# A router stage in one pass, a third PSUM bank for turned heads, and token lists shared between two engines

## The chip, the cores and the metric

One core of a Trainium2 chip runs the whole program. The metric is the time of one execution on the device, in microseconds (us), as the median of the runs shown; less is better. The core's engines run side by side and meet at semaphores: TensorE (PE, matmuls; PEld is its weight load), VectorE (DVE), ScalarE (ACT), GpSimd (POOL), and SyncE (SP), which here only issues transfers. TensorE's clock has two levels, 2.4 GHz (granted clock 1.0) and 1.2 GHz (0.5).

## What is computed

The reference takes x and a context of 8 batches x 256 tokens x 512 features through four stages. The change touches the first two:

```python
x = x + xattn(layernorm(x), ctx)            # 16 heads of 32; RMS norms on q and k; text part is empty
x = x + moe(layernorm(x))                   # 64 experts, the 8 best of each token
x = x + memory_attention(layernorm(x), ctx, mask)
x = x + ternary_ffn(layernorm(x))           # 512 -> 1408 -> 512

def moe(x):                                 # x: 2048 tokens x 512
    scores = softmax(x @ gate_weight.T)     # 64 scores a token
    topk_w, topk_idx = top_k(scores, 8)
    topk_w = topk_w / sum(topk_w)
    # each token goes to its 8 experts (512 -> 192 -> 512, silu), sorted by expert,
    # and the 8 results come back weighted
```

At the end of the attention the heads' outputs are multiplied by a 512x512 matrix and its bias `o_b` is added. The choice of experts depends on small differences of scores, so matmuls here are in float32, or in several passes of `fp32r` with each operand split into a high and a low part.

## The kernel before

The 2048 tokens are 16 tiles of 128 (`NT` = 16, P = 128), and 512 features are `DC` = 4 chunks of 128. Each stage is a block with one instruction stream for each engine; a barrier stands between blocks. Engines meet through `Steps`: a counter on which `done(instruction, name)` counts up and `wait(engine, unit, name)` waits for a named step of a unit. Each engine runs its own stream strictly in the order in which it is written.

- **project** (lines 89 to 243) makes qT, kT and V for 16 tiles. POOL normalises the tile's rows (L167 to L172) and otherwise waits for PE.
- **attend** (L246) has 32 units (8 batches x 4 groups of 4 heads), each in 2 slots of 2 heads. In slot s PE makes the scores `pS` (L312), in odd slots then the products `pO` of the unit two before (L333), and last it turns the heads of slot s-2 into `pT` (L323, on the page with `ident` as operand). DVE takes the smallest score of a row, `low` (L354), the reciprocals `inv` (L359) and copies three of four turned heads from PSUM (L368). ACT copies the fourth (L381), takes the exponentials `prob` (L388), and in even slots copies `pO` back into qT (L394, called "O"). POOL multiplies the probabilities by `inv` (L405). PSUM: two buffers pS of two banks each, two banks pT (head 0 and 1 of a slot), two banks pO, used by odd and even units. SP writes zeroes to unused rows and makes copies of the last stage's weights in DRAM.
- **route** (L419) has two passes. Pass one: POOL copies a tile of qT (L461), PE multiplies by `Wo` in float32 (L475), DVE adds the bias and then the sum to X and takes its statistics (L528 to L533). After all 16 tiles come the scales of the layernorm (16 aggregates, a root on ACT). Pass two, again over 16 tiles: ACT normalises (L510) into one of two buffers h, which is also stored to DRAM, PE turns h (L484), DVE copies it from PSUM (L546), PE makes 64 logits (L496), and DVE copies them, finds the 8 largest and marks them (L554 to L569). `Wo` and the bias are loaded when the block begins.
- **place** (L573) gives each pair of token and expert a slot in blocks of 128 rows, and makes for each block the list of its tokens: for each tile 8 one-hot matrices `hotr` (row, DVE, L741) and 8 step matrices `hotb` (block, ACT, L671), two buffers each, and 8 matmuls (L653) that wait for both. ACT also makes the high parts of the first three experts' weights (`wgu_high` L800, `wd_high` L805), two before its first step matrix and one after the ninth tile.
- **experts** and **finish** follow. In experts POOL names the first rows and gathers them (L925, L932); both stages are bound to what place and attend leave in memory.

## Time and profile before

| | us |
|---|---|
| median of 3 runs | 1686.16 |
| lowest and highest | 1680.62 and 1689.4 |
| the profiled execution, its own time | 1689.1 |
| its span (first to last instruction) | 1687.3 |

So 1.8 us of the profiled time lie outside its span, and the profiled execution is 2.9 us above the median. A row of a timeline gives start, duration, engine, source line, operation, what is written and read, a count of merged instructions, and in brackets the idle time before it and what ended that. A row of windows gives the stretch, its length, for each engine the busy time (and its instructions), then TensorE's granted clock, the share of time in which the DMA engines were busy, and GB/s. Start-to-start distances count, since the durations of successive instructions overlap by their pipelines.

### The profile page before, as it was taken

To read this page: it belongs to the slowest core of one execution; us is meant where nothing else is said; L and a number is where in the kernel's file an instruction comes from. 1 tells how busy PE (TensorE), PEld (TensorE's weight loads), DVE (VectorE), ACT (ScalarE), POOL (GpSimd) and SP (SyncE) were. 2 spreads that over 40 slices of the span, in tenths; PEclk is the share of its full clock that TensorE was granted. 3 is DMA by queue.
4 is the path that set the end of the run, shared out by engine and by line. 5 is a ranking of instruction groups with operands and counts; after the bars stand their busy time and mean duration, and the time that the engine had idled before them with its cause. 6 is when DMAs were issued, how large, how long until landed. Compare 5 with 4: busy or idle time off the path is not lost. (4 is left out here: it accounts for less than half of the span.)

```text
span 1687.3 us, 38047 instructions
## 1 busy us (share of the span) xinstructions
PE 1486.4 (88%) x8473; PEld 1166.0 (69%) x8474; DVE 1036.2 (61%) x2058; ACT 855.6 (51%) x1955; POOL 596.7 (35%) x680
## 2 busy tenths in 40 slices
PE   2999989998985479999999999999990679999999
PEld 1554556665453368888898899888980468888888
DVE  3343447776468847677767666666654556677632
ACT  0222257887025836576766666666650324444442
POOL 1111036776103132223223222322225476666322
PEclk9999969999986579999999999999995789999999
DMA  5000079000016148787878787777736554444200
GB/s 218 25 19 25 19 278 328 2 1 12 23 64 267 63 128 278 261 272 267 281 261 283 245 277 258 251 260 256 253 124 197 177 157 137 132 135 132 86 13 26
DMA packets 90388, 273.79 MB, mean 162 GB/s; under 512 B 12437, under 2 KB 12566, under 8 KB 89110
## 3 DMA queue, kind: packets, MB, share of 16 engines
q1 hardware_dynamic: 66214, 192.06, 31.9%
q0 software_dynamic: 23680, 77.61, 15.4%
q10 hardware_dynamic: 432, 3.41, 0.5%
q8 instruction: 24, 0.39, 0.1%
q14 instruction: 38, 0.31, 0.1%
HBM read 204.88 MB, written 76.81 MB: 167 GB/s over the span
## 5 line engine op out<-in xcount | busy, mean ns | idle before, releaser
L932 POOL DMA_INDIRECT xg<-h_rows,idx x168 | 184.4, 1098 | 466.2 <-PE m_x L960 457.1
L975 PE MATMUL m_g<-wgu_high,bxTh 128*128 x660 | 236.4, 358 | 4.2 <-DVE bxTl L1048 4.2
L975 PE MATMUL m_g<-wgu_low,bxTh 128*128 x660 | 223.9, 339 | 0.0
L975 PE MATMUL m_g<-wgu_high,bxTl 128*128 x660 | 223.7, 339 | 0.0
L1378 PE MATMUL f_g<-x4T_high,ffn_gu 128*128 128x256 f32 x704 | 176.9, 293 | 13.8 <-issue 12.1
L1378 PE MATMUL f_g<-x4T_low,ffn_gu 128*128 128x256 f32 x704 | 169.8, 282 | 0.0
L1048 DVE TENSOR_TENSOR bxTl<-m_x,bxTh 128x512 fp32r<-128x512 f32 x166 | 114.7, 691 | 84.8 <-ACT bxTh L1117 66.3
L810 DVE TENSOR_TENSOR wgu_low<-raw_gu,wgu_high x61 | 107.3, 1759 | 80.8 <-ACT wgu_high L800 64.5
L1135 ACT ACTIVATE y<-m_y 128x512 f32<-128x512 f32 x164 | 98.3, 599 | 110.7 <-PE m_y L995 89.1
L405 POOL TENSOR_TENSOR prob<-prob,inv 128x512 f32<-128x512 f32 x128 | 130.5, 1041 | 64.0 <-DVE inv L359 63.9
L1269 POOL DMA_INDIRECT G<-y_rows,slot x128 | 133.2, 1040 | 55.4 <-issue 49.4
L995 PE MATMUL m_y<-wd_high,hidTm 128*128 x328 | 144.7, 441 | 7.8 <-issue 6.1
L1378 PEld LDWEIGHTS f_g<-x4T_high,ffn_gu 128*128 128x128 f32 x704 | 135.1, 192 | 19.2 <-issue 16.5
L388 ACT ACTIVATE prob<-pS,low 128x256 f32<-128x256 f32 x256 | 118.0, 473 | 43.2 <-DVE low L354 43.2
L1378 PEld LDWEIGHTS f_g<-x4T_low,ffn_gu 128*128 128x128 f32 x704 | 135.0, 192 | 2.1 <-issue 1.7
L995 PE MATMUL m_y<-wd_low,hidTm 128*128 x328 | 130.1, 397 | 0.0
L975 PEld LDWEIGHTS m_g<-wgu_high,bxTh 128*128 128x128 f32 x660 | 124.5, 189 | 5.4 <-issue 4.6
L975 PEld LDWEIGHTS m_g<-wgu_low,bxTh 128*128 128x128 f32 x660 | 125.1, 189 | 0.0
L975 PEld LDWEIGHTS m_g<-wgu_high,bxTl 128*128 128x128 f32 x660 | 124.8, 189 | 0.0
L1117 ACT ACTIVATE bxTh<-m_x 128x512 fp32r<-128x512 f32 x166 | 99.0, 597 | 43.8 <-issue 42.3
L1432 DVE SCALAR_TENSOR_TENSOR X<-G,w,X 128x512 f32 (+1 forms) x128 | 106.1, 868 | 15.3 <-DMA G<-y_rows,slot 14.7
L1275 POOL TENSOR_TENSOR hT_low<-f_hid,hT_high 128x256 fp32r<-128x256 f32 x88 | 65.9, 750 | 119.5 <-ACT hT_high L1616 118.2
(235 smaller groups left out, 3155.9 us busy)
## 6 DMA issues: line engine op xcount, KB each, us to landing
raw_gu<-in_exp_gu SPq DMA_DIRECT2D x64, 768.0 KB, 6.8
y_rows<-y SPq DMA_DIRECT2D x164, 256.0 KB
raw_d<-in_exp_d SPq DMA_DIRECT2D x64, 512.0 KB, 7.6
y_rows<-zero SPq DMA_DIRECT2D x64, 256.0 KB, 3.4
ffn_gu<-ffn_gu_words SPq DMA_DIRECT2D x1, 5632.0 KB
X<-in_x SPq DMA_DIRECT2D x4, 1024.0 KB, 18.0
ctxT<-in_ctxT SPq DMA_DIRECT2D x16, 256.0 KB, 2.6
h_rows<-h SPq DMA_DIRECT2D x16, 256.0 KB, 2.0
```

Of the source, the lines that this page charges most:

```text
L388: e = eng.activation(prob[:, s % BUFS, i, h, :], pS[s % 2][:, i, h, :], ACT.Exp, bias=low[:, s % BUFS, i, h:h + 1], scale=-1.0, accum_out= ...
L405: poolN.done(eng.tensor_tensor(w, w, inv[:, s % BUFS, i, :].unsqueeze(2).to_broadcast([P, TPB, S]), ALU.mult), f"N{i}")
L810: eng.tensor_tensor(self.gu[1][:, at, :], self.raw_gu[:, at, :], self.gu[0][:, at, :].bitcast(F32), ALU.subtract).then_inc(self.s_low_gu, 1)
L932: eng.indirect_dma_start(xg[:, u, :].bitcast(F32), None, h_dram, bass.IndirectOffsetOnAxis(ap=idx[half][:, u:u + 1], axis=0)).then_inc(s_g ...
L975: m = eng.matmul(pg[u % 2][:, 0:2 * I], xT[l][:, u % 2, c, :], W.gu[r][:, buf * DC + c, :], start=c == 0 and n == 0, stop=c == DC - 1 and ...
L995: m = eng.matmul(py[par][:, :], left, right, start=n == 0, stop=n == 4)
L1048: dveX.done(eng.tensor_tensor(xT[1][:, u % 2, :, :], px[u % 2][:, :].rearrange("p (c n) -> p c n", c=DC), xT[0][:, u % 2, :, :].bitcast(F3 ...
L1117: actX.done(eng.activation(xT[0][:, u % 2, :, :], px[u % 2][:, :].rearrange("p (c n) -> p c n", c=DC), ACT.Copy), "xTh")
L1135: actY.done(eng.activation(y[:, u % 2, :], py[u % 2][:, :], ACT.Copy), "y")
L1269: eng.indirect_dma_start(G[:, i, k, :], None, y_dram, bass.IndirectOffsetOnAxis(ap=slot8[:, t, k:k + 1], axis=0)).then_inc(s_g[i][k], 16)
L1378: m = eng.matmul(pgu[f % 2][:, bass.ts(n, S)], Wgu[:, n, c, bass.ts(f, P)].bitcast(way), x[:, c, :].bitcast(way), start=c == 0 and part == ...
L1432: dveA.done(eng.scalar_tensor_tensor(X[:, t, :], G[:, i, k, :], w8[:, t, k:k + 1], X[:, t, :], ALU.mult, ALU.add), f"k{k}_{i}")
```

## The change

**project**: POOL adds `o_b` to each tile of X (a further `tensor_tensor` of 128x512), and waits for `rows`, now six rows, before it begins.

**attend**: `pT` has three banks, taken in turn by all heads, and `pO` has one bank in place of two. SP first loads the raw output weights; ACT makes their high parts in slots 8 to 11, POOL the low parts in slots 12 to 15.

**route**: one pass of 16 tiles. The product with the output weights is 12 `fp32r` matmuls of 512 columns a tile (high x high, high x low, low x high, for 4 chunks) in place of 4 in float32. ACT makes the high part of a tile of qT, DVE the low part. DVE adds the product to X in one operation, takes the statistics and one aggregate; POOL adds the epsilon and raises to -1/2; DVE makes the shift; ACT normalises (four buffers h) and also takes over the copy of the turned tile. The five operations on the logits stay on DVE.

**place**: `hotr` reads its row of numbers from SBUF in float16, in place of PSUM in float32. Of 8 step matrices DVE makes two for the first 12 tiles and one for the last 4, ACT the others. ACT makes one expert's high parts ahead of the step matrices, the others after tiles 1 and 3.

**experts**: POOL issues its first gathers ahead of the load of the number of used groups.

```diff
@@ project @@
+            eng.wait_ge(s_rows, 16)
...
+                    pool.done(eng.tensor_tensor(X[:, t, :], xc[:, :], rows[:, 5, :], ALU.add), "xb")
@@ attend @@
-        pT = [ps(f"pT{j}", [P, TPB, S]) for j in range(PAIR)]
-        pO = [ps(f"pO{j}", [P, S]) for j in range(2)]
+        pT, pO = [ps(f"pT{n}", [P, TPB, S]) for n in range(TBUFS)], ps("pO", [P, S])
...
+            eng.dma_start(Wraw[:, :, :], a["attn_wT"][3]).then_inc(s_wo, 16)
...
-                    turned(eng, (s - 1) // PAIRS, (s - 1) % PAIRS * PAIR + i)
+                    turned(eng, n - TBUFS)
...
-                actO.wait(eng, u - 2, "O")
+                actO.wait(eng, u - 1, "O")
...
+                if s in HIGHS:
+                    eng.wait_ge(s_wo, 16)
+                    eng.activation(Wo[0][:, s - HIGHS[0], :], Wraw[:, s - HIGHS[0], :], ACT.Copy).then_inc(s_high, 1)
                 if s % PAIRS == 0 and 0 <= s // PAIRS - 3 < UNITS:
                     u = s // PAIRS - 3
                     peO.wait(eng, u, "O")
-                    actO.done(eng.activation(qT[:, u % DC, bass.ts(u // DC, S)], pO[u % 2][:, :], ACT.Copy), "O")
+                    actO.done(eng.activation(qT[:, u % DC, bass.ts(u // DC, S)], pO[:, :], ACT.Copy), "O")
@@ route, TensorE and GpSimd @@
+                for c in range(DC):
+                    for n, (l, r) in enumerate(THREE):
+                        m = eng.matmul(po[t % 2][:, :], oT[l][:, t % 2, c, :], Wo[r][:, c, :],
+                                       start=c == 0 and n == 0, stop=c == DC - 1 and n == 2)
...
+            for s in range(NT + 2):
+                if s == 2:
+                    eng.wait_ge(s_r, 16)
+                if s >= 2:
+                    turn(s - 2)
+                if s < NT:
+                    project_out(s)
+                if s >= 2:
+                    choose(s - 2)
...
+                dveX.wait(eng, t, "mv")
+                actH.wait(eng, t - 2, "h")
+                pool.done(eng.tensor_scalar_add(lnp[:, t % 2, 0:1], mv[:, t % 2, 1:2], LN_EPS), "var")
+                pool.wait(eng, t, "var")
+                pool.done(eng.tensor_tensor(lnp[:, t % 2, 0:1], lnp[:, t % 2, 0:1], minus_half[:, :], ALU.pow), "rstd")
@@ place @@
+        on_vector = lambda t, k: k == K - 1 or (k == K - 2 and t < 3 * NT // 4)
...
-            for n in range(NWB - 1):
-                W.high_gu(eng, n, n)
-                W.high_d(eng, n, n)
+            W.high_gu(eng, 0, 0)
+            W.high_d(eng, 0, 0)
...
-                if t == NT // 2:
-                    W.high_gu(eng, NWB - 1, NWB - 1)
-                    W.high_d(eng, NWB - 1, NWB - 1)
+                if t in (1, 3):
+                    W.high_gu(eng, (t + 1) // 2, (t + 1) // 2)
+                    W.high_d(eng, (t + 1) // 2, (t + 1) // 2)
...
-                    m = eng.tensor_scalar(hotr[:, t % 2, k, :], prow[:, :], row_f[:, t, k:k + 1], tok_half[:, t:t + 1], ALU.is_equal, ALU.mult)
+                    m = eng.tensor_scalar(hotr[:, t % 2, k, :], it_row[:, :], row_f[:, t, k:k + 1], tok_half[:, t:t + 1], ALU.is_equal, ALU.mult)
+                    if on_vector(t, k):
+                        m = eng.tensor_scalar(hotb[:, t % 2, k, :], it_blk[:, :], blk_f[:, t, k:k + 1], 2.0, ALU.is_gt, ALU.mult)
@@ experts, GpSimd @@
-            groups = used_groups(eng, endb)
             name(0, 0)
             name(1, 1)
             for u in range(GB):
                 gather(0, u, 0)
+            groups = used_groups(eng, endb)
```

TensorE's stream in attend, from an odd slot's scores to the next even slot's, before. `a_dveT` and `a_actT` are the copies of turned heads, `a_poolN` the scaled probabilities, `a_actO` the copy of a product:

```order
L312 MATMUL pS1<-kT,qT 128x256 x3
L333 MATMUL pO1<-probT,V 32x256 [waits a_dveT,a_actT,a_actO]
L333 MATMUL pO1<-probT,V 32x256 x7
L323 MATMUL pT0<-ident,prob 128x128 [waits a_dveT,a_poolN]
L323 MATMUL pT1<-ident,prob 128x128 [waits a_dveT,a_poolN]
L312 MATMUL pS0<-kT,qT 128x256 [waits a_actE]
```

The same place in the changed kernel:

```order
L319 MATMUL pS1<-kT,qT 128x256 x3
L341 MATMUL pO<-probT,V 32x256 [waits a_dveT,a_actT,a_actO]
L341 MATMUL pO<-probT,V 32x256 x7
L331 MATMUL pT1<-ident,prob 128x128 [waits a_actT,a_poolN]
L331 MATMUL pT2<-ident,prob 128x128 [waits a_dveT,a_poolN]
L319 MATMUL pS0<-kT,qT 128x256 [waits a_actE]
```

The order is the same; the products go into the one bank `pO` every time, so their wait on `a_actO` is for the copy of the unit just before.

ACT's stream at the same place in the changed kernel (that of before differs only in the numbers of pO and pT):

```order
L396 ACTIVATE prob,tot<-pS0,low 128x256 [waits a_dveR,a_peT,a_dveM]
L396 ACTIVATE prob,tot<-pS0,low 128x256 x3
L405 ACTIVATE qT<-pO 128x256 [waits a_peO]
L396 ACTIVATE prob,tot<-pS1,low 128x256 [waits a_dveR,a_peT,a_dveM]
L396 ACTIVATE prob,tot<-pS1,low 128x256 x3
L389 ACTIVATE probT<-pT0 128x512 [waits a_peO,a_peT]
```

The copy that frees `pO` stands behind the four exponentials of the even slot.

DVE's stream in route, one tile of the second pass, before (`spares` and `low_bits` hold logits, masks and the best eight):

```order
L546 COPY hT<-ph0 128x512 [waits r_peL,r_peH]
L554 COPY spares<-pl1 128x64 [waits r_peL]
L557 MAX low_bits<-spares 128x8 [waits r_dveB]
L561 MATCH_REPLACE rest<-low_bits,spares 128x64 [waits r_dveB]
L563 TENSOR_TENSOR spares<-spares,rest 128x64 [waits r_dveB]
L569 TENSOR_TENSOR spares<-spares 128x64 [waits r_dveB]
```

One tile in the changed kernel:

```order
L572 SCALAR_TENSOR_TENSOR ln2_scale_shift<-ln2_mv,ln2_scale_shift 128x1 [waits r_pool]
L576 COPY spares<-pl1 128x64 [waits r_peL]
L557 TENSOR_TENSOR oT_low<-qT,oT_high 128x512 [waits r_peO,r_actO]
L581 MAX low_bits<-spares 128x8 [waits r_dveB]
L586 MATCH_REPLACE rest<-low_bits,spares 128x64 [waits r_dveB]
L590 TENSOR_TENSOR spares<-spares,rest 128x64 [waits r_dveB]
L598 TENSOR_TENSOR spares<-spares 128x64 [waits r_dveB]
L561 TENSOR_TENSOR X<-po0,X 128x512 [waits r_peO]
L564 BN_STATS ln2_stats<-X 128x6 [waits r_dveX]
L568 BN_AGGR ln2_mv<-ln2_stats 128x2 [waits r_dveS,r_pool,r_dveX]
```

The shift of a tile, which waits for POOL, is the first operation behind that tile's aggregate.

## Rows read from the trace of the kernel before

**Rows 1.** Windows: attend at half and at full clock, route, place.

```profile
219.50:261.70 42.20, 37.54 (x192) 24.28 (x192) 20.36 (x31) 23.39 (x88) 18.63 (x19) 0.56 0.95 356
261.70:418.80 157.10, 149.22 (x1345) 96.52 (x1344) 123.30 (x194) 127.26 (x492) 112.44 (x111) 1.00 0.20 68
418.80:524.60 105.80, 87.99 (x320) 52.82 (x320) 62.39 (x179) 14.30 (x18) 9.81 (x16) 0.88 0.14 54
524.60:594.60 70.00, 27.00 (x135) 17.28 (x135) 62.31 (x215) 54.98 (x138) 23.04 (x21) 0.50 0.44 177
```

**Rows 2.** Timeline of attend at the full clock, one unit of two slots.

```profile
300.57 1.13 PE L312 MATMUL pS<-kT,qT 32*128 32x256 f32 x8
301.75 1.23 DVE L354 TENSOR_REDUCE low<-pS 128x4 f32<-128x1024 f32 x1 [0.82 <-PE pS L312]
302.49 0.63 PE L323 MATMUL pT<-ident,prob 128*128 128x128 f32 x4 [0.21 <-ACT probT L381]
...
304.12 1.07 PE L333 MATMUL pO<-probT,V 128*32 128x256 f32 x16
304.82 0.40 ACT L394 ACTIVATE qT<-pO 128x256 f32<-128x256 f32 x1
305.12 1.09 PE L323 MATMUL pT<-ident,prob 128*128 128x128 f32 x8
306.14 1.13 PE L312 MATMUL pS<-kT,qT 32*128 32x256 f32 x8
```

**Rows 3.** Timeline of attend at the half clock, an odd slot.

```profile
256.40 2.08 PE L312 MATMUL pS<-kT,qT 32*128 32x256 f32 x8
...
258.40 1.94 PE L333 MATMUL pO<-probT,V 128*32 128x256 f32 x16
...
260.27 1.50 PE L323 MATMUL pT<-ident,prob 128*128 128x128 f32 x8
```

**Rows 4.** Timeline of route: pass one's start and one tile, then pass two.

```profile
424.33 25.88 PE L475 MATMUL po<-wo,oT 128*128 128x512 f32 x55 [6.01 <-DMA wo<-in_attn_wT]
...
451.51 0.69 DVE L530 TENSOR_TENSOR X<-X,add 128x512 f32 x1
...
452.44 0.69 DVE L533 BATCH_NORM_STATS2 ln_stats<-X  x1 [0.24 <-DVE X L530]
...
498.51 0.23 DVE L557 MAX8 low_bits<-spares 128x8 f32<-128x64 f32 x1
...
499.57 0.68 DVE L546 COPY hT<-ph 128x512 f32<-128x512 f32 x1
...
500.40 1.10 PE L496 MATMUL pl<-router_w,hT 128*128 128x64 f32 x8 [0.48 <-DVE spares L554]
```

**Rows 5.** Timeline of experts: `fp32r` matmuls of 512 columns.

```profile
702.70 0.39 PE L995 MATMUL m_y<-wd_high,hidTm 128*128 x1
702.93 0.39 PE L995 MATMUL m_y<-wd_low,hidTm 128*128 x1
```

**Rows 6.** Timeline of finish: the same two GpSimd operations on two columns.

```profile
1304.78 0.23 POOL L1281 TENSOR_SCALAR n_lnp<-n_mv 128x2 f32<-128x2 f32 x1
1305.09 0.73 POOL L1283 TENSOR_TENSOR n_lnp<-n_lnp,minus_half 128x2 f32<-128x2 f32 x1
```

**Rows 7.** Timeline of place.

```profile
532.95 0.23 DVE L722 TENSOR_SCALAR step<-blk_f 128x128 f32<-128x128 f32 x1
...
536.12 25.50 ACT L671 ACTIVATE hotb<-it_blk,step 128x201 f16<-128x201 f16 x72
...
549.20 2.64 DVE L741 TENSOR_SCALAR hotr<-prow,row_f,tok_half 128x128 f16<-128x128 f32 x8 [0.18 <-PE plist L653]
...
561.54 1.47 ACT L800 ACTIVATE wgu_high<-raw_gu 128x1536 fp32r<-128x1536 f32 x1
...
563.86 19.84 ACT L671 ACTIVATE hotb<-it_blk,step 128x201 f16<-128x201 f16 x56
```

**Rows 8.** Timeline of experts' start: the first gather.

```profile
596.27 1.23 POOL L932 DMA_INDIRECT xg<-h_rows,idx  x1 [0.89 <-POOL idx L925]
```

More of the change, by code:

```diff
@@ L416, in by_unit, with route @@
         one(t, t % unroll, lambda k, t=t: t + k < n)
-def route(nc, a, h_dram, X, qT, L, mask16, cum16, m8, ident):
+def route(nc, a, h_dram, X, qT, Wo, L, mask16, cum16, m8, ident):
+    tiles, HBUF = range(NT), 4
+    THREE = ((0, 0), (0, 1), (1, 0))
     with ExitStack() as ctx:
@@ L506, in _ @@
-            eng.wait_ge(s_ln, 1)
-            def norm(t, u):
-                peH.wait(eng, t - 2, "hT")
-                act.done(eng.activation(h[:, u, :], X[:, t, :], ACT.Identity, bias=lnp[:, t, 1:2], scale=lnp[:, t, 0:1]), "h")
-            for u in range(2):
-                norm(u, u)
-            with eng.Fori(1, NT // 2) as i:
-                for u in range(2):
-                    eng.wait_ge(s_h[u], i * 16)
-                    norm(i * 2 + u, u)
+            for x in (actO, actH, actT):
+                x.start(eng)
@@ L519, in _, with turned @@
+            def turned(t):
+                peH.wait(eng, t, "hT")
+                peL.wait(eng, t - 2, "l")
+                actT.done(eng.activation(hT[:, t % 2, :, :], ph[t % 2][:, :].rearrange("p (c n) -> p c n", c=DC), ACT.Copy), "hT")
+            high(0)
+            for s in range(NT + 2):
+                if s + 1 < NT:
+                    high(s + 1)
+                if 1 <= s <= NT:
+                    norm(s - 1)
+                if s >= 2:
+                    turned(s - 2)
         @block.vector
@@ L569, in one @@
                     dveB.done(eng.tensor_tensor(cum16[:, t, :], cum16[:, t - 1, :], mask16[:, t, :], ALU.add), "cum")
-            for t in range(NT):
-                one(t, t % 2, lambda k, t=t: t + k < NT)
+            low(0)
+            for s in range(NT + 3):
+                if 1 <= s <= NT:
+                    shift(s - 1)
+                b = s - 3
+                if b >= 0:
+                    logits(b)
+                if s + 1 < NT:
+                    low(s + 1)
+                if b >= 0:
+                    best(b)
+                    others(b)
+                    chosen(b)
+                    counted(b)
+                if s < NT:
+                    residual(s)
 def place(nc, a, W, Wgu, ffn_gu, s_ffn, L, mask16, cum16, m8, slot8, w8, blk_tok, endb, blk_tab, tab_dram):
```

175 lines of the change are left out of this document (87 added, 88 removed).

## The prediction

> **What bounds the kernel now.** I read the windows by stage first: the change touches attend, route and place, and what they take is 42.2 + 157.1, 105.8 and 70.0 us [rows 1]. Then I read the timeline of each, to see which wait ends last there.
>
> In attend at the full clock TensorE is busy in 149 of 157 us [rows 1]. One unit runs from one even slot's scores to the next, 300.57 to 306.14: 5.57 us [rows 2], and the slots from 261.7 on repeat it 26 times up to the last even slot. The only stall the rows show is one of 0.21 us at the second turned head, which waits for ACT's copy out of its bank. The products begin at 304.12, and ACT copies the products of the unit before at 304.82, after it: with two banks nobody minds [rows 2]. In the first 42 us the clock is at its half level (0.56 on average) [rows 1]; there scores take 2.00, products 1.87 (start to start, 256.40, 258.40, 260.27) [rows 3].
>
> In route TensorE bounds pass one and the clock is mostly up (0.88) [rows 1]; the block begins at 418.8 and its first matmul only at 424.33, after 6.01 us of waiting for the weights [rows 4]. In place TensorE is busy in 27 of 70 us at 0.50 [rows 1], and ACT's step matrices come without a gap: 72 in 25.50 us and 56 in 19.84, 0.354 each; DVE takes 2.64 for a tile's eight row matrices against ACT's 2.83 [rows 7].
>
> **attend: one bank for the products.** This is the edit that I take to decide. With one bank, the products of a unit wait for the copy of the unit before, and ACT does that copy behind the four exponentials of the even slot, which wait for `low`, which waits for that slot's scores. And the next even slot's scores stand behind the products on TensorE. That closes a loop, whose length is, from [rows 2]: scores to start of `low` 1.18 (300.57 to 301.75), start of `low` to the copy 3.07 (to 304.82, through the exponentials, without a gap), the copy 0.40, hand-over 0.12, products to turning 1.00 (304.12 to 305.12), turning to the next scores 1.02 (to 306.14). Sum 6.79, against 5.57 now: 1.22 more a unit, 26 times: **+31.7**. It does not depend on how early the heads are turned: nothing in the loop waits for `pT`. What is queued behind the waiting product is everything TensorE does next, the turning of the odd slot and the next scores, and behind those DVE and ACT.
>
> The third bank takes the 0.21 stall away, 26 x 0.21 = 5.5 at best. In the new loop it is worth nothing: there TensorE already has 1.2 us to spare in a unit.
>
> At the half clock the same loop costs 1.18 + 0.95 (scores 2.08 in place of 1.13) + 3.07 + 0.40 + 0.12 + 1.87 and about 1.9 for the turning [rows 2, 3] = 9.5, against 2 x 2.0 + 1.87 + 2 x 1.9 = 9.7 of TensorE's own work in a unit. So the first 42 us stay as they are.
>
> ACT's four high parts: those in slots 9 and 11 are beside the loop, those in 8 and 10 stand in it, ahead of the copy. 512 columns cost 0.5 to 0.6 by the 1536 columns in 1.47 [rows 7]: **+1.0** together. POOL's four low parts fit into its share (112 of 157 us busy [rows 1]), and the load is issued first on SP: 0; without that cover, 1 us each.
>
> **project.** POOL's extra addition lies beside TensorE and is needed only by route: 0. Only the first tile's could delay a matmul, by under 1 us.
>
> **route.** In the new pass a tile costs TensorE 12 x 0.233 = 2.8 [rows 5] for the product, about 0.5 for the turning (eight in 1.02 [rows 2]) and 1.1 for the logits [rows 4]: 4.4. DVE's stream costs more. From its rows [rows 4]: X to statistics 0.93, statistics 0.69, then a wait like the 0.24 there and the aggregate, 1.1 together; the low part 0.7 (the shape of L530); four operations on the logits 1.06 (498.51 to 499.57); the shift and the copy of the logits 0.2 each: 4.2. Then the loop passes POOL: epsilon 0.31 start to start and the power 0.73 [rows 6] and two hand-overs, 1.2, in which DVE stands, since the shift is next in its stream: 5.4 a tile. The power there has two columns, here one; a small POOL operation is 0.23 [rows 6], so the price is between 0.23 and 0.73, I take the row of the same operation, 0.73; the lower end would give 4.9 a tile, 7 us less in all. What is late, then, is DVE's loop, not TensorE.
>
> Sum: to the first aggregate 7.5 (ACT and DVE split the first tile, 1.5; 12 matmuls, 2.8 or 5.1 with the clock down; DVE 2), two tiles without logits at 4.1, 13 at 5.4, and 6.4 from the last aggregate (POOL 1.2, shift, normalising, turning, copy and logits 3.4, the last operations 1.8): 7.5 + 8.2 + 70.2 + 6.4 = 92.3 against 105.8: **-13.5**. The removed weight load (6.01 us [rows 4]) is in it.
>
> **place.** `step` is there at 533.18 [rows 7], and one expert's high parts end about 533.9. ACT then has 12 x 6 + 4 x 7 = 100 step matrices at 0.354 = 35.4 and two more experts at 2.32 (561.54 to 563.86) = 4.6: it ends at 573.9. Now it ends at 563.86 + 19.84 = 583.7: **-9.8**, if DVE keeps up. DVE begins at 536 as now. A row matrix costs 0.33 now, from PSUM; a float32 operation of 128 columns from SBUF takes 0.23 [rows 7]. At 0.23 for the row and 0.27 for the step matrix (201 columns) DVE needs 2.4 a tile for twelve tiles and 2.1 for four, and ends at 573, with ACT. If it gained nothing from SBUF it would need 3.4 a tile, end at 589, and the stage would lose 7. I take 0.23, since it is the nearest row. The DVE work behind its last tile, TensorE's last 8 matmuls and POOL's low parts move with it.
>
> The Trainium skill (VectorE: DVE Perf Modes, The perf-mode tier table) says that a one-source operation on 16-bit data in SBUF runs up to 4 elements a cycle and that any operand in PSUM lowers that; by its cycle table a row matrix would take 0.10 us, an estimate. DVE would then wait for ACT and the sum would be the same 9.8; against it speaks only that no row here has this form.
>
> **experts.** The first gather waits 0.89 us behind its list [rows 8]; ahead of the load of the register perhaps half of it goes: **-0.5** (0 to -0.9). The rest of experts and finish keeps its work and order.
>
> **Sum.** 31.7 + 1.0 - 13.5 - 9.8 - 0.5 = **+8.9**. On the profiled execution's own time, 1689.1, this gives 1698.0; the median shown is 1686.2, 2.9 lower, and on it the forecast is **1695**.
>
> **Rivals.**
> (a) The clock falls. In the new loop TensorE works 5.3 of 6.8 us. For it: route's mean of 0.88 and place's 0.50 show that it falls in stages with short work on TensorE, and attend ran 42 us at 0.56 before it came back up, though TensorE was busy in 37.5 of them [rows 1]. Against: in 261.7 to 418.8 it held 1.00 [rows 1]. Each unit at the half level costs 9.7 - 6.8 = 2.9 more, and route would be bound by TensorE at 8 a tile, 2.6 x 13 = 34 more. A third of attend, or half of route: +15 to +35, 1710 to 1730.
> The Trainium skill (TensorE: Matmul & The Clock Gate, A second HAM failure mode) describes this: short idle times between groups of matmuls, from cycling through PSUM, let the clock swing between its levels. By that rule the time is this rival's; the trace of before, at 1.00 with a stall of 0.21 in each unit, neither shows nor excludes it at 1.2.
> (b) The products do not wait as I say: the copy of `pO` is not held behind the exponentials, or the loop closes with less. Then attend gives 1.0 - 5.5 at best and the sum is -28: **1658 to 1665**, faster. Against it: in ACT's stream the copy is behind four exponentials, and the copy at 304.82 follows them without a gap [rows 2].
> (c) The loop is as computed, but route comes closer to TensorE's 4.4 a tile (power 0.23, fewer gaps): up to 13 more are saved, or the clock comes back in attend one or two units later, which spares 1.2 each: **1680 to 1690**, no change.
> (d) DVE becomes the bound in place (3.4 a tile): +17 on the sum, 1712, slower.
>
> **How the numbers follow.** My forecast with its own range of 1688 to 1702 has 0.50, about half of it on each side of +0.5%. (a) 0.15, (b) 0.08, (c) 0.20, (d) 0.07. About 0.5%, 8.4 us, is what a measurement can tell from no change. Slower by more: 0.28 + 0.15 + 0.05 = 0.48; within: 0.22 + 0.17 + 0.02 = 0.41; faster: 0.08 + 0.03 = 0.11. The range leaves out (b) and the far half of (a): 1676 to 1718.
>
> **What would show it.** In the profile after: units of attend at 6.8 in place of 5.57, with an idle time of about 1.2 before the products, released by ACT's copy; route some 92 us long, DVE's shift waiting for POOL about 1.2 us in each tile; ACT's last step matrix about 49 us behind the start of place, in place of 59. Wrong would be an attend of under 218 us, a route under 80 or over 105, or a granted clock of 0.5 in attend's second half.

## The result

The changed kernel takes 1707.8 us (median of 4 runs) against 1685.05 us for the kernel before (4 runs): a ratio of 1.0131, 95% interval [1.0097, 1.0164]. It is slower by more than the 0.5% that can be told, which was the likeliest outcome forecast. The time lies inside the range of 1676 to 1718 and 12.8 above the predicted 1695. The change itself, 22.7 us, is two and a half times the 8.9 that the sum gave. The profiled execution took 1709.99 us, with a span of 1708.1; the span of before was 1687.3, so the profiles differ by 20.8.

Windows of the changed kernel, cut where the stages now begin; columns as in [rows 1]: attend at half and at full clock, route, place.

```profile
219.50:270.00 50.50, 45.88 (x232) 29.11 (x232) 24.61 (x37) 28.02 (x103) 21.44 (x22) 0.54 1.00 368
270.00:453.80 183.80, 143.75 (x1308) 95.63 (x1304) 116.93 (x187) 126.84 (x480) 114.27 (x112) 0.99 0.13 45
453.80:538.40 84.60, 72.81 (x384) 58.63 (x384) 52.30 (x176) 29.51 (x48) 12.63 (x33) 0.93 0.14 52
538.40:612.80 74.40, 26.20 (x135) 16.45 (x135) 71.80 (x243) 44.17 (x108) 23.04 (x21) 0.52 0.42 166
```

Against [rows 1] this gives the balance:

| stage | before | after | difference | predicted |
|---|---|---|---|---|
| attend | 199.3 | 234.3 | +35.0 | +32.7 |
| route | 105.8 | 84.6 | -21.2 | -13.5 |
| place | 70.0 | 74.4 | +4.4 | -9.8 |
| experts and finish | 1092.7 | 1095.3 | +2.6 | -0.5 |
| span | 1687.3 | 1708.1 | +20.8 | +8.9 |

The sign came out as forecast because attend, the largest term, did. Two other terms were wrong by 14.2 and 7.7 us in opposite directions. That they cancelled in part, and the time so stayed well inside the range, is luck.

**attend after.** Timeline at the full clock, one unit, to be held against [rows 2]:

```profile
331.99 1.13 PE L319 MATMUL pS<-kT,qT 32*128 32x256 f32 x8
333.17 1.23 DVE L362 TENSOR_REDUCE low<-pS 128x4 f32<-128x1024 f32 x1 [0.82 <-PE pS L319]
...
336.24 0.40 ACT L405 ACTIVATE qT<-pO 128x256 f32<-128x256 f32 x1
...
336.69 1.07 PE L341 MATMUL pO<-probT,V 128*32 128x256 f32 x16 [1.48 <-ACT qT L405]
...
338.71 1.13 PE L319 MATMUL pS<-kT,qT 32*128 32x256 f32 x8
```

Scores at 331.99, `low` 1.18 later, the copy 3.07 after that, the products 0.45 after the copy's start and the next scores 2.02 after those: 6.72 us, against 5.57 before and 6.79 forecast. The idle time of 1.48 before the products is ended by ACT's copy.

**place after.** Timeline, to be held against [rows 7]:

```profile
549.66 14.05 DVE L784 TENSOR_SCALAR hotr<-it_row,row_f,tok_half 128x128 f16<-128x128 f16 x7
549.72 2.13 POOL L676 TENSOR_TENSOR marked<-spares,order 128x1024 f32<-128x1024 f16 x1 [6.24 <-DVEq L780]
551.81 3.42 POOL L855 TENSOR_TENSOR wgu_low<-raw_gu,wgu_high 128x1536 fp32r<-128x1536 f32 x1
555.20 2.33 POOL L860 TENSOR_TENSOR wd_low<-raw_d,wd_high 128x1024 fp32r<-128x1024 f32 x1
557.50 3.41 POOL L855 TENSOR_TENSOR wgu_low<-raw_gu,wgu_high 128x1536 fp32r<-128x1536 f32 x1
560.87 2.33 POOL L860 TENSOR_TENSOR wd_low<-raw_d,wd_high 128x1024 fp32r<-128x1024 f32 x1
...
564.22 1.64 DVE L784 TENSOR_SCALAR hotr<-it_row,row_f,tok_half 128x128 f16<-128x128 f16 x7
564.35 1.53 PE L698 MATMUL plist<-hotb,hotr 128*128 128x201 f16 x8 [21.64 <-DVE hotb L786]
565.92 4.37 ACT L715 ACTIVATE hotb<-it_blk,step 128x201 f16<-128x201 f16 x12 [12.23 <-PE plist L698]
```

Seven row matrices take 14.05 us from 549.66, just as long as POOL works without a break (549.72 to 563.20), and seven others take 1.64 as soon as POOL is done. TensorE, idle since 542.7, waits until 564.35 for the first tile (21.64 us), and ACT, which may be two tiles ahead, waits 12.23 for TensorE. The same happens once more, 6.86 us for seven, when POOL makes the third expert's low parts at 571.74. ACT's last step matrix ends 64 us behind the start of place; before it was 59, forecast 49.

### The profile page after: what moved, and what is told of

Its sections match the earlier page's. It is cut to its first block and busy times, and to the rows that moved or that the text cites. A ratio compares the mean times of both kernels' runs of the same rounds, so it can differ in the third digit from the quotient of the medians.

```text
span 1708.1 us, 37961 instructions
## 1 busy us (share of the span) xinstructions
PE 1471.2 (86%) x8537; PEld 1172.6 (69%) x8538; DVE 1034.0 (61%) x2083; ACT 863.4 (51%) x1959; POOL 626.4 (37%) x717
## 5 line engine op out<-in xcount | busy, mean ns | idle before, releaser
L977 POOL DMA_INDIRECT xg<-h_rows,idx x168 | 188.7, 1123 | 463.4 <-PE m_x L1005 455.5
L1423 PE MATMUL f_g<-x4T_high,ffn_gu 128*128 128x256 f32 x704 | 176.8, 293 | 13.3 <-issue 11.2
```

What stands on the lines that cost most here:

```text
L977: eng.indirect_dma_start(xg[:, u, :].bitcast(F32), None, h_dram, bass.IndirectOffsetOnAxis(ap=idx[half][:, u:u + 1], axis=0)).then_inc(s_g ...
L1423: m = eng.matmul(pgu[f % 2][:, bass.ts(n, S)], Wgu[:, n, c, bass.ts(f, P)].bitcast(way), x[:, c, :].bitcast(way), start=c == 0 and part == ...
```

## Experiments

Theories. For attend: the single `pO` bank closes a loop through ACT's copy. For place: VectorE's new operations, which read and write SBUF alone, stand still beside POOL's. The rivals are named with each run. A ratio is to the kernel before, run beside that variant, with its 95% interval in brackets; where only one execution of a variant was taken, there is no ratio. Stages are compared by their first landmarks: ACT's first high part of route, POOL's `ones` for place, VectorE's `blk_tok` at its end. By these, place is 73.8 us in the changed kernel and 68.6 before.

**1. Two banks again** (`e1_two_banks`).

```diff
-    SLOTS, BUFS, TBUFS = UNITS * PAIRS, 4, 3
+    SLOTS, BUFS, TBUFS = UNITS * PAIRS, 4, 2
...
-        pT, pO = [ps(f"pT{n}", [P, TPB, S]) for n in range(TBUFS)], ps("pO", [P, S])
+        pT, pO = [ps(f"pT{n}", [P, TPB, S]) for n in range(TBUFS)], [ps(f"pO{j}", [P, S]) for j in range(2)]
...
-                actO.wait(eng, u - 1, "O")
+                actO.wait(eng, u - 2, "O")
...
```

> The changed kernel with the buffers of attend as they were (two pT banks, two pO banks), all else of the change kept. Theory (the single pO bank closes a loop through ACT's copy): attend falls from 234 us back to 199 to 201, its unit from 6.72 to 5.6, the time from 1707 to about 1673, a ratio to the kernel before of 0.992. Rival (the parts of the output weight that ACT and POOL now make inside attend, or a longer half clock of TensorE, cost the time there): attend stays at 225 or more and the ratio at 1.008 or more.

Measured: 0.9943 [0.9918, 0.9969]; attend 201.8 us, the unit 5.56 (scores at 300.64 and 306.20). The banks cost the time, not the parts of the weight that ACT and POOL make there.

**2. The copy ahead of the exponentials** (`e2_early_copy`), still three `pT` banks and one `pO`.

```diff
@@ attend, ScalarE @@
+                if s % PAIRS == 0 and 0 <= s // PAIRS - 3 < UNITS:
+                    u = s // PAIRS - 3
+                    peO.wait(eng, u, "O")
+                    actO.done(eng.activation(qT[:, u % DC, bass.ts(u // DC, S)], pO[:, :], ACT.Copy), "O")
                 if s < SLOTS:
                     dveM.wait(eng, s, "M")
...
-                if s % PAIRS == 0 and 0 <= s // PAIRS - 3 < UNITS:
-                    u = s // PAIRS - 3
-                    peO.wait(eng, u, "O")
-                    actO.done(eng.activation(qT[:, u % DC, bass.ts(u // DC, S)], pO[:, :], ACT.Copy), "O")
```

> The changed kernel with three pT banks and one pO bank, but ACT's copy of pO put ahead of the four exponentials of its slot instead of behind them. Theory (the loop closes only because the copy stands behind the exponentials): the wait of the products on the copy goes from 1.5 us to under 0.2, the unit to 5.6, the time to about 1673 (ratio 0.992), as with two banks. If the third pT bank is worth something once the loop is open, it is at most the 0.21 us that the turned heads waited in 26 units, 5 us, so 1668 to 1673. Rival (one bank is too few wherever the copy stands, since the products then wait for the copy and the copy for the products): unit 6.2 or more, ratio 1.005 or more.

Measured: 0.9896 [0.9849, 0.9942], attend 187.0 us. Timeline at the full clock, one unit:

```profile
299.86 1.13 PE L319 MATMUL pS<-kT,qT 32*128 32x256 f32 x8
...
304.01 1.17 PE L331 MATMUL pT<-ident,prob 128*128 128x128 f32 x8
...
304.58 0.40 ACT L393 ACTIVATE qT<-pO 128x256 f32<-128x256 f32 x1
305.10 1.13 PE L319 MATMUL pS<-kT,qT 32*128 32x256 f32 x8
305.38 0.47 ACT L400 ACTIVATE prob<-pS,low 128x256 f32<-128x256 f32 x1 [0.40 <-DVE low L362]
...
306.17 1.07 PE L341 MATMUL pO<-probT,V 128*32 128x256 f32 x16
```

The copy (304.58) now lies in the time in which ACT waits for `low`, 1.6 us before the products, which wait for nothing. One bank is enough; where the copy stood was the fault. The unit is 5.24 us (299.86 to 305.10), 0.32 under two and two banks. That is more than the 0.21 that I had allowed the third bank; run 3 tells what brings it.

**3. Which of the two edits gives the 5.24** (`e8_early_two_turned`): the early copy, with only two `pT` banks.

```diff
-    SLOTS, BUFS, TBUFS = UNITS * PAIRS, 4, 3
+    SLOTS, BUFS, TBUFS = UNITS * PAIRS, 4, 2
```

> The changed kernel with ACT's copy of pO ahead of the exponentials, one pO bank, and only two pT banks. It tells apart what made attend 187.6 us with the early copy and three pT banks, where two and two banks gave 202. Theory (the third pT bank brings it, the unit goes from 5.56 to 5.24 us): here the unit is 5.5 to 5.6 again, attend 199 to 203 us, the ratio 0.993 to 0.996. Rival (the order on ACT brings it, the third bank nothing): unit 5.24, attend about 188, ratio 0.990.

Measured: 0.9947 [0.9917, 0.9977], attend 200.3. Timeline, one unit:

```profile
303.17 0.66 PE L331 MATMUL pT<-ident,prob 128*128 128x128 f32 x4
...
304.02 0.63 PE L331 MATMUL pT<-ident,prob 128*128 128x128 f32 x4 [0.20 <-ACT probT L389]
304.58 1.13 PE L319 MATMUL pS<-kT,qT 32*128 32x256 f32 x8
...
310.15 1.13 PE L319 MATMUL pS<-kT,qT 32*128 32x256 f32 x8
```

The stall of 0.20 is back and the unit 5.57: it is the third bank that brings the 5.24. The row names 0.20 of wait, but split in two the turning loses more: from its start to the next scores 1.41 here (303.17 to 304.58), 1.09 in one go in run 2 (304.01 to 305.10). 26 x 0.33 = 8.6 us, or 0.5%, which is the difference of the two ratios. The attend stages of the two profiles differ by more, 13.3 us: in this one the granted clock came back at about 261, in run 2's at about 242 (last section).

**4. VectorE reads PSUM** (`e3_marks_psum`): ACT first copies both rows there, as the kernel before did with one.

```diff
+            eng.activation(pblk[:, :], it_blk[:, :], ACT.Copy)
+            eng.activation(prow[:, :], it_row[:, :], ACT.Copy).then_inc(s_row, 1)
...
-                    m = eng.tensor_scalar(hotr[:, t % 2, k, :], it_row[:, :], row_f[:, t, k:k + 1], tok_half[:, t:t + 1], ALU.is_equal, ALU.mult)
+                    m = eng.tensor_scalar(hotr[:, t % 2, k, :], prow[:, :], row_f[:, t, k:k + 1], tok_half[:, t:t + 1], ALU.is_equal, ALU.mult)
...
-                        m = eng.tensor_scalar(hotb[:, t % 2, k, :], it_blk[:, :], blk_f[:, t, k:k + 1], 2.0, ALU.is_gt, ALU.mult)
+                        m = eng.tensor_scalar(hotb[:, t % 2, k, :], pblk[:, :], blk_f[:, t, k:k + 1], 2.0, ALU.is_gt, ALU.mult)
```

> The changed kernel with both rows that VectorE compares in place (row marks and block numbers) read from PSUM in float32 instead of SBUF in float16; the split of the block steps between ACT and VectorE is kept. Theory (VectorE's float16 SBUF form stands still while POOL subtracts the low parts of the weights; the PSUM form does not, as in the kernel before): the stretches of 14.05 and 6.86 us for seven operations go, one row mark takes 0.33 us and one block step about 0.41 throughout, so 128 x 0.33 + 28 x 0.41 = 53.7 us, the last list ends at about 604 instead of 612.7 and place is 66 us instead of 74.6: about -8, 1699, ratio 1.008. Rival (the stall comes from ACT's or TensorE's side, or from the block steps that VectorE got): place stays at 74 us or grows, since every operation is dearer, ratio 1.013 or more.

Measured: 1.0125 [1.0087, 1.0162], place 72.4. Timeline, the same stretch of place as above:

```profile
549.86 2.33 DVE L787 TENSOR_SCALAR hotr<-prow,row_f,tok_half 128x128 f16<-128x128 f32 x7 [0.22 <-DVE slot L781]
549.85 2.14 POOL L676 TENSOR_TENSOR marked<-spares,order 128x1024 f32<-128x1024 f16 x1 [6.24 <-DVEq L782]
...
553.09 2.32 DVE L787 TENSOR_SCALAR hotr<-prow,row_f,tok_half 128x128 f16<-128x128 f32 x7
```

The mechanism is as the theory says: beside the same POOL operations seven row matrices take 2.33 instead of 14.05, and POOL is no slower. My -8 us was not right, nor the ratio of 1.008. VectorE needed 50 us for the marks and steps where I had 53.7, and was done at about 600; but in the changed kernel it had been done at about 601. I had set the end of the lists in one kernel against the end of the stage, 8 us later, in the other. The dearer form cost nearly what the stall had: place is 1.4 us shorter.

**5. POOL's low parts after the lists** (`e4_low_late`).

```diff
@@ place, GpSimd, behind marked @@
+            dveH.wait(eng, NT - 1, "hot")
             for n in range(NWB):
                 W.low_gu(eng, n, n)
```

> The changed kernel in which POOL begins the low parts of the first three experts' weights only after VectorE's last row mark of place. Theory (POOL's subtractions hold VectorE's float16 operations up): the first seven row marks take 1.7 to 4 us instead of 14.05 (only POOL's marked, 2.1 us, is left beside them), no later seven take over 2.2, ACT becomes the bound and the last list ends 49 to 52 us behind the start of place instead of 74; the low parts (17 us) then follow, so the whole time is within 10 us of the changed kernel's. Rival (POOL's work has nothing to do with the stall): the 14 us and the 6.9 us stay and place ends where it did.

Measured: 1711.7 us (one run). Timeline of VectorE and POOL, the lists' first tile and what comes behind the lists:

```profile
550.17 3.59 DVE L785 TENSOR_SCALAR hotr<-it_row,row_f,tok_half 128x128 f16<-128x128 f16 x7
550.23 2.13 POOL L676 TENSOR_TENSOR marked<-spares,order 128x1024 f32<-128x1024 f16 x1 [6.24 <-DVEq L781]
...
562.56 26.92 ACT L716 ACTIVATE hotb<-it_blk,step 128x201 f16<-128x201 f16 x76
...
588.36 3.42 POOL L856 TENSOR_TENSOR wgu_low<-raw_gu,wgu_high 128x1536 fp32r<-128x1536 f32 x1 [36.00 <-DVE hotb L787]
588.80 3.54 DVE L799 TENSOR_SCALAR key<-spares 128x1024 int32<-128x1024 int32 x1
...
592.37 3.24 DVE L802 TENSOR_TENSOR key<-key,marked 128x1024 f32<-128x1024 int32 x1
594.49 4.40 POOL L856 TENSOR_TENSOR wgu_low<-raw_gu,wgu_high 128x1536 fp32r<-128x1536 f32 x1
595.64 2.13 DVE L804 MAX8 found<-key 128x8 f32<-128x64 f32 x16
```

The first seven take 3.59 (1.64 and the 2.1 of `marked`), and ACT, never held up, ends at 589.48, 50.6 us behind the start of place at 538.9, where the prediction had 49. So the term was right but for POOL. Yet place is only 2.7 us shorter, 71.1 for 73.8, since moving POOL's work only moves the collision: VectorE's next operations, 0.69 and 1.23 us long in the changed kernel, now take 3.54 and 3.24, and POOL's subtraction 4.40 instead of 3.42. MAX8, beside that subtraction, takes its 2.13 as ever.

**6. The row in float32** (`e6_rows_f32`).

```diff
-        it_i, it_row, it_blk = sb("it_i", [P, NTAB + 1], I32), sb("it_row", [P, P], F16), sb("it_blk", [P, NTAB + 1], F16)
+        it_i, it_row, it_blk = sb("it_i", [P, NTAB + 1], I32), sb("it_row", [P, P]), sb("it_blk", [P, NTAB + 1], F16)
```

> The changed kernel with the row marks' source as float32 in SBUF instead of float16; the block steps' source stays float16. Theory (what stands still beside POOL's subtractions is any fast form of VectorE that reads and writes SBUF alone, not the float16 form): the first seven row marks again take about 14 us and another seven about 6.9, one undisturbed mark 0.2 to 0.3 us. Rival (the float16 form alone is held up): no such stretch, the first seven take about 2, the last list ends some 10 us earlier than in the changed kernel.

Measured: 1712.2 us (one run). Timeline:

```profile
544.55 14.15 DVE L784 TENSOR_SCALAR hotr<-it_row,row_f,tok_half 128x128 f16<-128x128 f32 x7
...
559.24 1.87 DVE L784 TENSOR_SCALAR hotr<-it_row,row_f,tok_half 128x128 f16<-128x128 f32 x7
...
566.48 7.19 DVE L784 TENSOR_SCALAR hotr<-it_row,row_f,tok_half 128x128 f16<-128x128 f32 x7
```

14.15 and 7.19, with 1.87 undisturbed: the float32 source in SBUF is held up just so. What counts is that nothing lies in PSUM, not the type. Place is 77.6 us here, 3.8 more than in the changed kernel, since each undisturbed seven are dearer (1.87 for 1.64).

**7. POOL's work twice** (`e9_low_twice`).

```diff
             for n in range(NWB):
...
+                eng.tensor_tensor(W.gu[1][:, g, :], W.raw_gu[:, g, :], W.gu[0][:, g, :].bitcast(F32), ALU.subtract).then_inc(s_twice, 1)
+                eng.wait_ge(s_twice, 2 * n + 1)
                 W.low_gu(eng, n, n)
...
+                eng.tensor_tensor(W.d[1][:, d, :], W.raw_d[:, d, :], W.d[0][:, d, :].bitcast(F32), ALU.subtract).then_inc(s_twice, 1)
+                eng.wait_ge(s_twice, 2 * n + 2)
                 W.low_d(eng, n, n)
```

> The changed kernel in which POOL makes each low part of the first three experts' weights in place twice over (the same values written again). Theory (VectorE stands still as long as POOL subtracts): POOL works 2.1 + 23 us without a break in the first stretch and 11.5 in the second; the first seven row marks take 25.5 to 27 us instead of 14.05, a later seven about 12.5 instead of 6.9, place is 90 to 92 us instead of 73.8 and the whole time 16 to 18 us above the changed kernel's. Rival (each of VectorE's operations loses a fixed time at POOL's start, or only POOL's first operations matter): the stretches stay below 20 and 9 us, and place below 84.

Measured: place 89.7 us, 15.9 more than in the changed kernel, for 17.2 more of POOL's work (expected 90 to 92, the rival below 84). The stretches did not fall as I had written (25.5 to 27 and about 12.5 for seven), since I expected the seven to be held for all of it. Timeline of VectorE:

```profile
555.82 3.48 DVE L794 TENSOR_SCALAR hotb<-it_blk,blk_f 128x201 f16<-128x201 f16 x1
559.21 3.55 DVE L792 TENSOR_SCALAR hotr<-it_row,row_f,tok_half 128x128 f16<-128x128 f16 x1
562.69 2.40 DVE L794 TENSOR_SCALAR hotb<-it_blk,blk_f 128x201 f16<-128x201 f16 x1
```

One VectorE operation slips in between two of POOL's, and then the next one waits for the whole of POOL's (3.42 or 2.33). So the first seven were through after 13.95 us, five POOL operations, and the operations behind them were held for the rest; where POOL worked on the third expert, seven took 4.78. The whole time, 1711.6, did not grow by 16: attend was 226.1 us in this execution and 233.6 in the changed kernel's, with the same code (the granted clock came back at about 242 here and at about 271 there), and the stages behind place were 6 us shorter. One execution cannot tell 16 us by its total; by its place stage it does.

**8. Route alone** (`e5_route_alone`): run 1, with the place stage of the kernel before put back as a whole.

> The changed kernel with two pT and two pO banks in attend and with the place stage of the kernel before, so that of the change the new route stage (with what it needs in project and attend) is left alone. Theory (the parts add up: route -21 us as in the profile of the changed kernel, place +5): 5 us less than the run with two banks in attend, a ratio to the kernel before of 0.991, route 84.6 us long, place 69. Rival (route's gain is given back behind it, by weights that land later or by the clock): ratio 0.995 or more.

Measured: 0.9882 [0.9817, 0.9947]; route 82.9 us, place 68.5. Route's gain of 21 us stands in its stage. The time agrees, 1.2% of 1684 is 20, but its interval allows 9 to 31, and attend was 8.5 us shorter in this execution than in run 1's with the same code. Against run 1 the old place is worth 0.6%, but the intervals overlap; in the stages it is 5.4 us.

**9. Sources by what POOL does** (`e7_early_mixed`, and the same kernel once more as `e11_early_mixed_again`): with run 2's early copy, VectorE reads PSUM for the first seven tiles and SBUF for the other nine, for the row marks as in the diff and for the block steps likewise. The split of the block steps changes with it: VectorE makes one a tile in the first seven tiles and two in the other nine.

```diff
-        on_vector = lambda t, k: k == K - 1 or (k == K - 2 and t < 3 * NT // 4)
+        FROM_PSUM = 7
+        on_vector = lambda t, k: k == K - 1 or (k == K - 2 and t >= FROM_PSUM)
...
-                    m = eng.tensor_scalar(hotr[:, t % 2, k, :], it_row[:, :], row_f[:, t, k:k + 1], tok_half[:, t:t + 1], ALU.is_equal, ALU.mult)
+                    m = eng.tensor_scalar(hotr[:, t % 2, k, :], (prow if t < FROM_PSUM else it_row)[:, :], row_f[:, t, k:k + 1], tok_half[:, t:t + 1], ALU.is_equal, ALU.mult)
```

> The changed kernel with ACT's copy of pO ahead of the exponentials, and in place with VectorE's two sources read from PSUM for the first seven tiles (while POOL subtracts) and from SBUF in float16 for the other nine; VectorE makes one block step a tile in the first seven and two in the other nine. Theory: no stretches; VectorE takes 7 x 2.9 + 9 x 2.14 = 39.6 us from the start of its marks, ACT 103 x 0.354 + 7.5 = 44 from its own, so the last mark comes 9 to 12 us earlier than in the changed kernel and place is 63 to 65.5 us; together with the ratio of 0.9896 of the early copy alone this is 0.982 to 0.984, about 1648 against 1677. Rival (the weights that POOL or ACT prepare, or TensorE at its half clock, bound place as soon as VectorE does not): place 70 us or more, ratio 0.987 or more.

> The version with the early copy of pO and the mixed sources in place once more, in five rounds, for a narrower interval than 0.9834 [0.977, 0.9897]. Theory (the parts add: 0.9896 with the early copy alone, 12 us less in place): 0.9825 to 0.984. The time at which TensorE's clock comes back up in attend differs from execution to execution and may move it by 0.3% either way.

Measured: 0.9834 [0.977, 0.9897] and 0.9849 [0.9815, 0.9884]; place 61.8 and 61.7 us, 12 less than in the changed kernel, the upper end of the 9 to 12 worked out. Both ratios are below the early copy alone (0.9896), by 0.6 and 0.5% where 12 us are 0.7%; the intervals overlap, so the gain is shown by the stage.

**10. The mixed sources without the early copy** (`e10_mixed_only`).

> The changed kernel with the mixed sources in place (PSUM for the first seven tiles, SBUF for the rest, one and then two block steps a tile on VectorE), and attend exactly as changed. Theory (the stall behind POOL is all that kept place from its gain): place 61.8 us instead of 73.8, the ratio to the kernel before 1.0131 - 12 / 1684 = 1.006, which is the changed kernel's as the prediction had it. Rival (the early copy in attend was needed for place to gain): ratio 1.010 or more.

Measured: 1.0094 [1.0059, 1.0128]; place 61.7, attend 234.2. The stage gained its 12 us without the early copy, so the rival falls there. The ratio is higher than 1.006, and the interval just holds that value; against the changed kernel's 1.0131 it is 0.4% lower where 12 us are 0.7%, which the two intervals cover. In this execution the granted clock was back at about 253, and TensorE then stood for 2.00 us before the products, since one of ACT's high parts stands ahead of the copy there. Behind it the clock was at its half level again, to about 279. Timeline, then the window:

```profile
257.92 1.07 PE L341 MATMUL pO<-probT,V 128*32 128x256 f32 x16 [2.00 <-ACT qT L405]
```

```profile
260.00:278.00 18.00, 17.82 (x93) 11.12 (x91) 9.06 (x14) 8.80 (x31) 6.12 (x6) 0.50 1.04 365
```

Attend, at 234.2, is still only 0.6 us longer than in the changed kernel's profile.

**11. Filling VectorE's wait in route** (`e12_fill_wait`), on the version of 9.

```diff
@@ route, VectorE @@
-                if 1 <= s <= NT:
-                    shift(s - 1)
                 b = s - 3
                 if b >= 0:
                     logits(b)
                 if s + 1 < NT:
                     low(s + 1)
+                if 1 <= s <= NT:
+                    shift(s - 1)
```

> The version with the early copy and the mixed sources, in whose route stage VectorE copies the logits and makes the next low part before the shift, in the 0.97 us in which it waited for POOL's power. Theory (VectorE's stream, with the wait on POOL in it, sets route's 4.58 us a tile, and nothing else is close below): the wait falls to 0.2 or less, a tile takes 4.23 to 4.4 us (TensorE has 0.36 + 2.8 + 0.94 = 4.1 of its own; from one product through the shift, ACT's two operations and the logits to the product after the next there are 8.46 us for two tiles), route is 3 to 5 us shorter than the 84.9 to 85.2 of the same kernel without it, and the ratio 0.001 to 0.003 lower, inside the interval. Rival (the loop is closed over ACT and TensorE, not by VectorE's stream): 4.58 a tile stays, route 84.5 us or more.

Measured: 0.983 [0.9773, 0.9887], route 83.8 against 85.1 (3 to 5 us less expected), and 4.56 us a tile (eight from 433.64 to 470.14) against 4.58. The tile moved by far less than the wait that was filled. Timeline, one tile of the changed kernel, then one of this:

```profile
482.96 0.18 DVE L568 BATCH_NORM_AGGREGATE ln_mv<-ln_stats 128x2 f32<-128x6 f32 x1
...
483.23 0.21 POOL L477 TENSOR_SCALAR ln_scale_shift<-ln_mv 128x1 f32<-128x1 f32 x1 [3.72 <-DVE ln_mv L568]
...
483.52 0.56 POOL L479 TENSOR_TENSOR ln_scale_shift<-ln_scale_shift,r_minus_half 128x1 f32<-128x1 f32 x1
...
484.11 0.16 DVE L572 SCALAR_TENSOR_TENSOR ln_scale_shift<-ln_mv,ln_scale_shift 128x1 f32<-128x1 f32 x1 [0.97 <-POOL ln_scale_shift L479]
```

```profile
440.04 0.18 DVE L568 BATCH_NORM_AGGREGATE ln_mv<-ln_stats 128x2 f32<-128x6 f32 x1
...
440.25 0.68 DVE L557 TENSOR_TENSOR oT_low<-qT,oT_high 128x512 fp32r<-128x512 f32 x1
440.31 0.70 POOL L477 TENSOR_SCALAR ln_scale_shift<-ln_mv 128x1 f32<-128x1 f32 x1 [3.24 <-DVE ln_mv L568]
...
441.70 0.16 DVE L572 SCALAR_TENSOR_TENSOR ln_scale_shift<-ln_mv,ln_scale_shift 128x1 f32<-128x1 f32 x1 [0.77 <-POOL ln_scale_shift L479]
```

VectorE's low part, with two sources in SBUF, began first (440.25), and POOL's one-column operation beside it took 0.70 instead of 0.21. The collision works in both directions. VectorE still waited 0.77 us before the shift, which came 1.66 us behind the aggregate instead of 1.15, and the chain of two tiles over ACT and TensorE that the expectation names grew from 8.46 by that 0.5 to 9.0, 4.5 a tile, close to the 4.56. VectorE's stream and TensorE's product are now equally late: `X` starts at 443.02, where both VectorE's last logits operation (442.77, 0.19 long) and the product's last matmul (442.60, 0.39 long) end. So by the tile the rival won (4.58 stays); by the stage neither did, since the theory had 3 to 5 us less and the rival 84.5 or more. What the order would have gained without the collision isn't shown.

## Why the prediction was right, and where it was not

**attend: right.** The loop was named with its members and came out at 6.72 for 6.79; the third bank was worth nothing in it and the products waited 1.48. Runs 1 and 2 confirm the cause from two sides. The copy and the hand-over took 0.45 where the sum had 0.40 + 0.12, of which no row had shown the 0.12. Of the 2.3 us more than the sum, none is in the unit. The half clock lasted to about 271, where before it ended at about 261; a unit at the half clock takes 9.7 us and one at the full clock 6.72, so these 10 us cost about 3, an estimate. When the clock returns differs between executions (below). ACT's high parts, forecast at 1.0, fell into the half clock here and made the products wait 0.18 twice; in run 10 one stood in the loop at the full clock, and the wait was 2.00 instead of 1.48. Step "5.5 at best" for the third bank: 8.6 in truth, since the row of the wait (0.21) is not all that a split group of matmuls loses.

**Rivals.** (a), the clock falling in the new loop, did not happen in this profile: 0.99 in the window from 270 to 453.8, with a stall of 1.48 in each unit. The Trainium skill (TensorE: Matmul & The Clock Gate, A second HAM failure mode) tells of such a swing in another kernel, and the prediction took it as a rule; the trace does not agree for this pattern. But the rival is not empty. In runs 5, 6 and 10, whose attend code is the same, the granted clock fell back to 0.50 once for 10 to 20 us, each time behind a wait of 2.00 before the products; in run 7 it stayed at 1.00 behind two such waits, and in run 1, without the loop, it fell for 3 us behind a wait of 1.17. Whether the waits are the cause isn't shown. (b) is what run 2 makes of the kernel. (c) came partly true, (d) nearly: VectorE did become the bound in place, by a mechanism that I had not seen.

**route: the right mechanism, the wrong size.** The step that was off is "5.4 a tile": 4.58. The changed kernel's rows of one tile, start to start, with my terms put the same way: `X` to statistics 0.83 (I had 0.93), to the aggregate 0.73 (0.93, with a wait of 0.24 that did not come), to the shift, over POOL, 1.15 (1.38), shift, logits and low part to the first of the four 0.82 (1.10), these four and the gap to `X` 1.05 (1.06). POOL's power on one column took 0.56, between my 0.23 and 0.73. The largest part, 0.28, comes from adding durations where the next operation starts about 0.1 us before the last one ends. 13 tiles x 0.82 = 10.7 less; the start and the end of the pass gave 3 of it back, part of that at the half clock (matmuls 0.43 apart until 458.6). Run 8 shows the same gain without the new bank counts in attend and the new place.

**place: the step that failed.** "I take 0.23, since it is the nearest row" was right as a price: seven take 1.64, 0.23 each. The estimate of 0.10 that I had quoted by the Trainium skill was not; it comes from the cycle table (VectorE: DVE Perf Modes, The TRN2 errata), 58 cycles and 128/4 more at 0.96 GHz, which is 0.094. The trace does not agree with it for operations of 128 columns. What failed is "POOL's low parts move with it", which made POOL a bystander. The operations were held up by 14.05 - 1.64 + 6.86 - 1.64 = 17.6 us. Of these, 13.6 reached ACT's last step matrix (64.2 us behind the start of place, 50.6 in run 5): ACT stood 12.23 and 2.88 us for TensorE here and 1.76 there, and made its other high parts meanwhile. Runs 4 to 7 settle the cause: the stall goes with PSUM sources (4), goes when POOL waits (5), stays with float32 (6), and place grows by nearly all that POOL is given more (7).

The Trainium skill has the rule that I should have weighed (SBUF — State Buffer, Who interferes with whom): VectorE's second pair of SBUF ports is also GpSimd's only one, taken by whichever starts first for a whole instruction; on VectorE's side it concerns copies and `tensor_scalar` with all in SBUF in their two-port modes, and, beside a GpSimd operation that reads SBUF, operations with two SBUF inputs, while one with at most one SBUF input outside those modes stays clear of it. The traces agree in each point that they touch: 0.33 a row matrix from PSUM, 2.13 for MAX8 (one SBUF input), and both directions in run 11. The trace of before had it too, in a stage that I did not read for this: finish. VectorE and POOL there, twice two accumulations of two SBUF inputs, with and without POOL's low part beside them:

```profile
1374.49 0.73 POOL L1275 TENSOR_TENSOR hT_low<-f_hid,hT_high 128x256 fp32r<-128x256 f32 x1 [2.35 <-ACT hT_high L1616]
1374.54 1.89 DVE L1432 SCALAR_TENSOR_TENSOR X<-G,w,X 128x512 f32 x2
...
1408.03 1.40 DVE L1432 SCALAR_TENSOR_TENSOR X<-G,w,X 128x512 f32 x2
```

1.89 against 1.40 for the same work. A group whose longest member is over twice its median (here 1.63 against 0.75 for L1432) is where to look; that the longest is of this cause isn't shown.

**experts: the right size, in another place.** First gather, to be held against [rows 8]:

```profile
614.47 1.23 POOL L977 DMA_INDIRECT xg<-h_rows,idx  x1 [0.84 <-POOL idx L970]
```

The wait of 0.89 that was to be halved stayed, at 0.84. What went is time ahead of it: from the last list (`blk_tok`, 612.35) to POOL's `idx` there are 0.97 us (613.32) instead of 1.79 (593.27 to 595.06), since `idx` too now comes before the load, so 2.1 to the gather instead of 3.0: -0.9, the upper end, partly by luck. The +2.6 of the later stages can't be put down to the change: from the last list on, the fourteen profiled executions took 1089 to 1103 us, and the variants with the changed kernel's own code there differ by as much.

## The version that beats both

Early copy, three `pT` banks, new route, mixed sources: 0.9834 and 0.9849, some 26 us under the kernel before and 50 under the changed one. With run 11's order 0.983 [0.9773, 0.9887], not to be told from it.

## What to carry to other kernels

Before giving up a second buffer, follow the loop that it leaves: when the reader of the single buffer stands in its engine's queue behind work that depends on the writer's next step, the loop is closed; moving the reader ahead of that work opened it at no cost here. A faster form of an operation has to be priced beside what its neighbours do at that moment: on VectorE a `tensor_scalar` with all in SBUF, or an operation with two SBUF inputs, waited for POOL's operations; a `tensor_scalar` from PSUM and MAX8 did not. Sum a stream by the spacing of starts, not by durations.

## What the runs showed of the hardware

- VectorE's `tensor_scalar` with source and result in SBUF, float16 or float32, waits for POOL's subtractions, one whole POOL operation at a time (up to 3.55 us for one of 0.23); from PSUM it takes 0.33 beside the same. The other way round, POOL's epsilon took 0.70 instead of 0.21 beside a VectorE subtraction of 0.68.
- Filling VectorE's wait on POOL with a two-input operation in SBUF lengthened the chain over POOL from 1.15 to 1.66 us (run 11).
- Early in attend the granted clock falls to 0.50 (0.66 from 220 to 230, 0.50 from 230 to 260 in the changed kernel), with TensorE busy nearly all the time (37.5 of 42.2 us before), and the time at which it returns differs with the same code: attend was 201.8 us in run 1 and 193.3 in run 8, whose attend code is the same. In the fourteen profiles it came back at about 242 (five), 252 (three), 261 (four) or 271 (two), one unit of 9.7 us apart. Window of run 2 up to that point; from 243.0 to 406.5 it is at 1.00:

```profile
219.50:243.00 23.50, 19.97 (x105) 13.29 (x105) 11.58 (x17) 14.12 (x52) 10.57 (x11) 0.56 1.01 359
```

  Until then each unit takes about 9.7 us instead of 5.2 to 6.7. Between those two runs this is 0.5% of the total, more than several of the edits here are worth; the stages in the trace tell such edits apart, the totals hardly.
- A stall of 1.48 us in every 6.72 left the granted clock at 0.99 over 184 us. Behind waits of 2.00 us it fell to 0.50 in three executions (runs 5, 6, 10) and not in a fourth (run 7).
